# Shared feed-forward units of width 352: 64 columns of gate and of up in one chunk, 32 of each for both halves of the tokens side by side; gathered rows shared out anew

## The reference, cut to what matters

```
x = x + tanh(g_xattn[l]) * xattn_l(layernorm(x), ctx)
x = x + tanh(g_ffn[l]) * ffn_l(layernorm(x))
# ffn of layer 1 (top 4 of 16) and of layer 2 (top 6 of 16): expert width 352, shared width 704
shared = silu(x @ sw_gate) * (x @ sw_up) @ sw_down
routed = sum over the chosen experts e of w_e * (silu(x @ gate_e) * (x @ up_e)) @ down_e
# ffn of layer 0 (top 2 of 16): width 256, gelu, with biases, two shared experts
```

## Time and profile before

| | before |
|---|---|
| median of 3 runs | 2452.13 us (2451.92 to 2452.92) |
| profiled execution | 2452.95 us, its span 2451.2 us |
| PE busy | 2275.7 us, 93% of the span |
| DVE / ACT / POOL busy | 982.8 / 713.6 / 373.9 us |
| mean granted PE clock | 0.973 of full speed |
| stretch of the router stage, layer 1 and layer 2 | 1160.7 to 1219.7, 1591.9 to 1655 us |
| stretch of the combine stage, layers 0, 1, 2 | 763 to 805, 1488 to 1581, 2069 to 2143 us |

### The profile page before, as it was taken

How to read it: one execution, slowest core, us unless ns; L and a number is a source line. 1 busy time by engine, 2 the same in 40 slices (tenths; PEclk the granted TensorE clock), 3 DMA queues, 4 the chain that set the end, 5 groups by cost and what they waited for, 6 DMA issues and landing times. The chain is left out here.

```text
span 2451.2 us, 33056 instructions
## 1 busy us (share of the span) xinstructions
PE 2275.7 (93%) x9625; PEld 1366.0 (56%) x9626; DVE 982.8 (40%) x2525; ACT 713.6 (29%) x1674; POOL 373.9 (15%) x513
## 2 busy tenths in 40 slices
PE   7899999998898899998999999699999999699898
PEld 4444444444664566666456564245656555356587
DVE  5645455444333433335612224771222222602375
ACT  2445353630111566666011110301111110051221
POOL 6100000000122100000011114401111112500061
PEclk9999999998999999999999999799999999899999
DMA  9401010022774100001456555143444452561220
GB/s 345 128 1 35 0 35 0 0 81 95 254 245 137 31 18 6 14 14 53 132 163 201 197 182 168 48 142 111 148 147 148 151 166 78 145 235 38 90 91 31
DMA packets 169969, 263.72 MB, mean 108 GB/s; under 512 B 13134, under 2 KB 106702, under 8 KB 169373
## 3 DMA queue, kind: packets, MB, share of 16 engines
q1 hardware_dynamic: 139869, 186.06, 23.1%
q0 software_dynamic: 15040, 49.30, 6.7%
q10 hardware_dynamic: 14976, 27.27, 2.9%
HBM read 212.78 MB, written 49.81 MB: 107 GB/s over the span
## 5 line engine op out<-in xcount | busy, mean ns | idle before, releaser
L1369 PE MATMUL bank<-f2r_wd,f2b_hT 128*128 (+1 forms) x300 | 137.2, 593 | 1.4 <-DVE f2b_hT L1480 1.4
L1350 PE MATMUL bank<-f2r_wg,f2b_xT 128*128 x400 | 129.2, 467 | 2.0 <-issue 2.0
L1350 PE MATMUL bank<-f2r_wu,f2b_xT 128*128 x400 | 127.0, 460 | 0.0
L1467 DVE TENSOR_TENSOR f2b_h<-bank,f2b_acted 128x352 f32<-128x352 f32 x50 | 26.2, 525 | 203.1 <-PE bank L1350 203.1
L1813 PE MATMUL bank<-l0a_vo,l0a_zT 128*128 128x512 f32 x224 | 101.5, 596 | 3.2 <-DVE l0a_zT L1978 3.2
L1350 PEld LDWEIGHTS bank<-f2r_wu,f2b_xT 128*128 128x128 f32 x400 | 76.4, 191 | 42.8 <-issue 0.7
L1877 ACT ACTIVATE l0a_p<-l0a_p,l0a_low 112x375 f32<-112x375 f32 x128 | 77.2, 607 | 77.5 <-DVE l0a_low L1969 76.4
L1959 DVE CUSTOM_DVE_ANT_0 l0a_p<-bank,xn 112x375 f32<-112x375 f32 x128 | 70.3, 549 | 67.5 <-PE bank L1785 35.6
L1783 PE MATMUL bank<-l_kvcT,xnT 128*112 128x375 f32 x256 | 92.3, 482 | 5.0 <-ACT xnT L1906 5.0
L2154 PEld LDWEIGHTS bank<-l1w_v,ctxT 128*125 128x125 f32 x768 | 88.7, 188 | 8.4 <-issue 0.6
L1350 PEld LDWEIGHTS bank<-f2r_wg,f2b_xT 128*128 128x128 f32 x400 | 73.1, 193 | 35.1 <-issue 4.0
(11 more groups left out here) (410 smaller groups left out, 4281.3 us busy)
## 6 DMA issues: line engine op xcount, KB each, us to landing
slot_rows<-zeros SPq DMA_DIRECT2D x2, 7424.0 KB, 37.7
slot_rows<-f2b_y ACTq DMA_DIRECT2D x50, 256.0 KB, 3.5
f1r_wg<-in_l_wg SPq DMA_DIRECT2D x16, 704.0 KB, 4.3
f1r_wu<-in_l_wu SPq DMA_DIRECT2D x16, 704.0 KB, 5.6
f2r_wg<-in_l_wg SPq DMA_DIRECT2D x16, 704.0 KB, 4.3
f2r_wu<-in_l_wu SPq DMA_DIRECT2D x16, 704.0 KB, 5.6
xn<-in_l_w_ffn SPq DMA_DIRECT2D x11, 768.0 KB, 4.4
l_raw<-in_l_w_ffn SPq DMA_DIRECT2D x11, 768.0 KB, 4.4
```

What stands on the lines that cost most here:

```text
L1350: mm = pe.matmul(bank[:, 0:width], xT[:, v, k, :], w[:, bass.ds(at, 1), k, :].rearrange("p o f -> p (o f)"), start=(k == 0), stop=(k == KD ...
L1369: mm = pe.matmul(bank_y[v][:, :], hT[0:fn, v, c, :], wd[0:fn, bass.ds(at, 1), c, :].rearrange("p o f -> p (o f)"), start=(c == 0), stop=(c ...
```

## The change

The chunk of 96 columns is replaced. Its first 64 columns of the gate and the same 64 of the up lie side by side in one chunk of 128 columns, so that four matmuls make both (a **tail**, one for each half). The last 32 columns of gate and 32 of up make a chunk of 64, and the two halves of the tokens are made in the same four steps: half 0 into partitions 0 to 63 of the bank, half 1 into partitions 64 to 127 (the **rest**, one for both halves). The host lays gate and up out in one array, which is loaded in one transfer where there were two. In layers 1 and 2 there are now 7 pieces: chunk 0 and chunk 1 of half 0, the rest, the tail of half 0, chunk 0 and chunk 1 of half 1, the tail of half 1. The rest needs two activations and two multiplies (of 32 partitions each). Layer 0 keeps its four pieces.

```diff
+        self.whole = whole = width // 128
+        self.pieces = [("chunk", 0, c) for c in range(whole)]
+        if width % 128:
+            self.pieces += [("rest", None, None), ("tail", 0, None)]
+        self.first_half = len(self.pieces)
+        self.pieces += [("chunk", 1, c) for c in range(whole)]
+        if width % 128:
+            self.pieces.append(("tail", 1, None))
+        self.columns = [KD * HALF * (2 if kind == "chunk" else 1) for kind, half, c in self.pieces]
...
+    def make_piece(self, pe, q, gu, h_done, g_done, u_done, between=None):
+        if q >= 2:
+            pe.wait_ge(h_done, q - 1)
...
+        elif kind == "tail":
+            for k in range(KD):
+                mm = pe.matmul(first[:, 0:HALF], gu[:, k, whole * 256:whole * 256 + 128], tokens(k, half),
+                               start=(k == 0), stop=(k == KD - 1))
+            mm.then_inc(g_done, 1)
+        else:
+            for k in range(KD):
+                for half in range(2):
+                    mm = pe.matmul(first[64 * half:64 * half + 64, 0:HALF], gu[:, k, whole * 256 + 128:whole * 256 + 192],
+                                   tokens(k, half), start=(k == 0), stop=(k == KD - 1))
+            mm.then_inc(g_done, 1)
...
+            act.wait_ge(h_done, q)
+            act.activation(acted[64:96, 0, :], bank[0:32, 0:HALF], self.func)
+            act.activation(acted[64:96, 1, :], bank[64:96, 0:HALF], self.func).then_inc(act_done, 1)
...
+            dve.tensor_tensor(hT[64:96, last, 0:HALF], up[32:64, 0:HALF], acted[64:96, 0, :], ALU.mult)
+            dve.tensor_tensor(hT[64:96, last, HALF:NT], up[96:128, 0:HALF], acted[64:96, 1, :], ALU.mult).then_inc(h_done, 1)
```

```diff
+    late = MOST_TILES if top_k > 4 else 0
...
             def product(b):
-                pe.wait_ge(h_done, FC if b < HALF_TILES else PIECES)
+                pe.wait_ge(h_done, FIRST if b < HALF_TILES else PIECES - 1)
...
+                    if b == HALF_TILES and c == FC - 1:
+                        pe.wait_ge(h_done, PIECES)
...
-                columns = 2 * KD * HALF * pieces + FC * D * products
-                return min(len(gathers), len(gathers) * columns //
-                           (2 * KD * HALF * PIECES + FC * D * (HALF_TILES if state else TILES)))
+                columns = sum(shared.columns[:pieces]) + FC * D * products
+                due = len(gathers) - late
+                return min(due, due * columns // (sum(shared.columns) + FC * D * HALF_TILES))
...
             for b in range(HALF_TILES, TILES):
                 add(b)
-                combine_some(share(PIECES, b + 1))
+                if late:
+                    combine_some(added[0] + 1)
```

More of the change, by code:

```diff
@@ L493, in gate_up @@
             def gate_up(q, between=None):
-                half, (f0, fn) = q // FC, chunks[q % FC]
-                if q >= 2:
-                    pe.wait_ge(h_done, q - 1)
-                for weight, out, done in ((wg, s.bank[2 * (q % 2)], g_done), (wu, s.bank[2 * (q % 2) + 1], u_done)):
-                    if between and weight is wu:
-                        between()
-                    for k in range(KD):
-                        mm = pe.matmul(out[0:fn, 0:HALF], weight[:, k, f0:f0 + fn],
-                                       s.xnT[:, k, half * HALF:(half + 1) * HALF], start=(k == 0), stop=(k == KD - 1))
-                    mm.then_inc(done, 1)
+                shared.make_piece(pe, q, gu, h_done, g_done, u_done, between)
             def ranks_and_counts():
@@ L745, in _ @@
                 hidden(q)
[L746 to L747 removed]
+                for i in range(2 * q - 4, min(2 * q - 2, 2 * top_k)):
+                    one_hots(i)
             for i in range(2 * PIECES - 4 if PIECES > 4 else 2, 2 * top_k):
@@ new lines, in __init__, with chunks_until, load @@
+        if width % 128:
[5 more added lines that the diff above has]
+        self.columns = [KD * HALF * (2 if kind == "chunk" else 1) for kind, half, c in self.pieces]
+    def chunks_until(self, q):
+        return sum(kind == "chunk" for kind, half, c in self.pieces[:q + 1])
+    def load(self, eng, i):
+        width, (gu, wd), done = self.width, self.w[i], self.loaded[i]
+        eng.dma_start(gu[:, :, :], self.gate_up[i].rearrange("(k p) f -> p k f", p=128)).then_inc(done, 16)
+        load_down(eng, (None, None, self.w_down), E + i, width, wd, done)
@@ L989, in _ @@
         def _(pe):
[L990 removed]
+            pe.wait_ge(shared.loaded[1], 16 * 3)
             def piece(q):
[L993 to L1000 removed]
+                shared.make_piece(pe, q, gu, h_done, g_done, u_done)
             def product(b):
[L1003 removed]
+                pe.wait_ge(h_done, FIRST if b < HALF_TILES else PIECES - 1)
                 if b >= BANKS:
@@ L1009, in product @@
                 mm.then_inc(y_done, 1)
-            for q in range(FC + 1):
+            for q in range(FIRST + 1):
                 piece(q)
@@ L1016, in _ @@
                 product(b)
-            for q in range(FC + 1, PIECES):
+            for q in range(FIRST + 1, PIECES):
                 piece(q)
-                if state and q == 4:
+                if state and q == FIRST + 1:
                     state.rows_product(pe)
@@ L1120, in _ @@
                 add(b)
-                combine_some(share(FC + 1, b + 1))
-            for q in range(FC + 1, PIECES):
+                combine_some(share(FIRST + 1, b + 1))
+            for q in range(FIRST + 1, PIECES):
                 hidden(q)
-                if state and q == 4:
+                if state and q == FIRST + 1:
                     state.copy_rows(dve)
@@ L2879, in halves_swapped, with shared_parts @@
     return np.ascontiguousarray(w.reshape(w.shape[0], n, 2, width // 2)[:, :, ::-1].reshape(w.shape))
+def shared_parts(width):
+    whole = width // 128 * 128
+    cuts = [0, whole] + ([whole + 64, width] if width > whole else [])
+    return [slice(a, b) for a, b in zip(cuts, cuts[1:])]
 def lay_out(i):
@@ L2937, in lay_out @@
     d["l2_wd"] = c(np.concatenate([f["L2_ffn_w2"].transpose(0, 2, 1), f["L2_ffn_sw2"].T.reshape(2, 352, D)]))
+    for layer in range(3):
+        d[f"l{layer}_shared_gu"] = c(np.concatenate([w[:, :, columns] for columns in shared_parts(d[f"l{layer}_wg"].shape[-1])
+                                                     for w in (d[f"l{layer}_wg"][E:], d[f"l{layer}_wu"][E:])], axis=-1))
     d["l2_decay"] = f["L2_xattn_decay"].reshape(1)
```

133 lines of the change are left out of this document (69 added, 64 removed).

## The result

| | before | changed |
|---|---|---|
| median (20 runs each) | 2452.24 us (2448.48 to 2461.35) | 2459.22 us (2450.59 to 2467.89) |
| profiled execution, its span | 2452.95 us, 2451.2 us | 2457.10 us, 2455.4 us |
| ratio | | 1.0023, 95% interval 1.0013 to 1.0032 |

The forecast was 2451 us and "within 0.2%", its range 2443.5 to 2456.5. The measured time lies 2.7 us above the range, 7.0 us above before.

A forecast was written before the change was run, and what follows sets the result against it. PE, busy 93% of the span, was taken as the bound, with what follows PE deciding the combines of layers 1 and 2. -3.0 - 2.6 + 5.1 + 1.6 - 2.4 = -1.3 us, about 2451 us; range 2443.5 to 2456.5.

The forecast's parts named there:

- combine 0: Layer 0's combine: last product starts earlier and no row is left behind the last piece's, so DVE ends sooner; -2.6 us.
- router 1: Layer 1's router: PE pauses 5.7 us ahead of its first listing, the tail adds 3.0, a slow clock follows; +5.1 us.
- combine 1: Layer 1's combine: PE's last piece ends sooner, so DVE's recurrence begins sooner, with gathers landed by then; -3.0 us.
- router 2: Layer 2's router: PE's saving had in part (-2.9), then tail +3.0, last tables +0.6, clock 0.9; +1.6 us.
- combine 2: Layer 2's combine: with late signals ending at 2123.3 as before, less work lies behind the last product; -2.4 us.
- the hold: Layer 2's combine: signal of PE's finished matmuls some 13 us late, PE standing 11.39 us; assumed to recur once (0.50).
- the hold is gone: Rival, 0.32: no late signal in layer 2's combine, which gathers then bound; stage -7.2, total -6.1, 2446 us.
- held twice: Rival, 0.10: the seventh piece's signal in layer 2's combine also waits for the last gathers; +8.9, total +7.6, 2460 us.
- the clock: Routers: PE runs at half speed behind a pause; +1.6 us in layer 1 (bounds 0 and 3.1), 0.9 in layer 2.
- The rest in 3.0 us: Shared units' rest: narrow matmuls in two groups of output partitions run beside each other, costing 3.0 us, not 6.0.

The follow-up runs named there:

- e3: Kernel before the change, with POOL waiting ahead of gathers 12, 24 and 36 of combine stages until the one before has landed; 2457.41 us, 1.0010 of before.
- e2: Changed kernel, with POOL waiting ahead of gathers 12, 24 and 36 of combine stages until the one before has landed; 2461.51 us, 1.0029 of before.
- e6: e1 with every one-hot table ahead of DVE's table chain, and POOL gaps before gathers 12 and 24 (combine 1) or 20 (combine 2); 2441.96 us, 0.9945 of before.
- e7: e6 with the last two multiplies of layer 2's combine made at once, ahead of the rows that lay between them; 2440.94 us, 0.9945 of before.
- e8: Changed kernel, fetching only the first 64 of 128 rows from the ninth gather of each combine stage on; 2462.06 us, 1.0034 of before.
- e9: Changed kernel, with POOL writing a 64-column tile of zeros behind each gather from the ninth on in combine 1; 1.0038 of before.
- e1: Changed kernel, with the routers' four chunks of 128 ordered ahead of the rest and the two tails; 1.0042 of before.
- e4: Changed kernel, with the old way of sharing out the gathered rows behind the products; 2459.74 us, 1.0026 of before.

## Why the prediction was wrong

Over the traces whose stage is the same program, the mean of each stage moved as follows (before: its two traces, and e3 for the stages that gaps don't touch; changed: its two traces, and the experiments that left the stage alone, six traces for the routers, five for each of the combines of layers 1 and 2).

| stage | forecast | measured | from |
|---|---|---|---|
| combine 0 | -2.6 | -2.8 | 44.1 to 41.3 |
| router 1 | +5.1 | +6.2 | 61.8 to 68.1 |
| combine 1 | -3.0 | +1.0 | 93.9 to 94.8 |
| router 2 | +1.6 | +2.3 | 64.0 to 66.3 |
| combine 2 | -2.4 | -0.4 | 73.5 to 73.0 |
| sum | -1.3 | +6.3 | medians: +7.0 |

The two combines of layers 1 and 2 scatter by 3 to 8 us, so their means are rough; the others are firm within about 1 us.

- **Combine 1, -3.0: this step failed.** It said that the stage "gains what PE gains up to its last piece". PE's work did shrink by 3 us, and with gaps in the gathers the stage does, nearly (91.0, e2, e6, e7). The term that I had put at nothing is what the gathers do to PE in this stage. In seven of the eight traces of the changed combine without gaps, e8 and e9 among them, PE's matmuls were drawn out around the state product (16.4 to 20.7 us from there to the first down product, 14.4 with gaps), and signals came late in all eight and in before's second. I had written that "the same gathers in layer 1 show none", from one trace.
- **Combine 2, -2.4: failed likewise.** The forecast took the hold as a fixed event that ends at 2123.3. It wanders: ahead of the last four products PE stands 11.39 us in before's first trace and 3.67 in its second, and over five traces of the changed stage combine 2 took 70.9 to 78.8 us. Even with one hold, as forecast (the changed kernel's first trace), the stage moved by -1.5: DVE needs 2.5 us for each of the last four tiles (addition, row, statistics), as long as a product, and ended 3.1 us behind the last product, not 2.4. Against "the hold is gone" I argued that three runs agreed within 1.0 us, "so the hold isn't a chance event". Seventeen more runs of before spread over 13 us. The rival "held twice" (10%, 2460 us) is partly what the changed kernel's second trace shows: the seventh piece's signal came 8.8 us late, when POOL had issued its last gather, though the first hold lies at the fourth piece and not at the sixth. That the median, 2459 us, lies next to this rival's is luck: over the traces combine 2 did not get longer.
- **Router 1, +5.1: right in its mechanism, mis-sized in the clock.** The pause was 5.46 us (forecast 5.7), the tail behind it 3.0. The slow stretch cost 3.5 us instead of 1.6; my bound of 3.1 was too low as well, since the listing ahead of the piece runs slowly too. That e1 takes the pause away and finds another one where DVE is late next, and that e6, without either, needs 58.8 us, shows the order to be the cause and not the pieces.
- **Router 2, +1.6 against +2.3: right in its mechanism**, the clock again above what I had taken (the fifth piece's gate took 4.70 us from start to start instead of 3.08, 1.6 lost, forecast 0.9).
- **Combine 0: right**, and e4 gives 2.2 of the 2.8 to the rows.
- **The rest in 3.0 us: right.** Sixteen records took 3.15 us from start to start. The Trainium skill ("TensorEngine Tiling (Array Packing)", section "Tiling Modes") has the engine drain when the mode changes; the wide records on either side were at most 0.1 us further apart than without a change, as the earlier trace rows had said.

So the sum came out 7.6 us low: 4.0 in combine 1, 2.0 in combine 2, 1.1 and 0.7 in the clock of the routers, less 0.2. The first is PE's delay beside the gathers; the second, a difference of means over stages that scatter by 8 us, is the hold as far as I can tell. With the clock alone mis-sized the forecast would have read +0.5, still "no change".

**What was shown and what wasn't.** Shown: with gaps after every twelfth gather the worst delay of a signal is 2.7 us (e2, e3), while each of the ten traces without added gaps has one of 4.7 us or more; gaps also bring combine 1 of the changed kernel to 91.0 us in three kernels out of three; half the data does not (e8). The late signals around a pause of POOL have come 3.4 us after its last issue at the latest; some came while it still issued, and a pause of 2.2 us in e1's combine 1 did not let the state product's signal go (its last matmul ended at 1515.05, the signal came at 1520.75). Not shown: how much of e6's 12 us each of its three edits brings, since no kernel has the new order with the late tables alone. Open: what in POOL's issuing holds PE's signals, why PE's own matmuls are drawn out around the state product of the changed combine 1 and not before the change, and whether a wider step without a full gap would do; e9 didn't reach that.

## What to carry to other kernels

When a change takes work from one engine ahead of a meeting with another, look at who arrives last: work that was cover becomes a pause, and on PE a pause is paid twice, since what follows it runs at half the clock (5.5 us of pause, 3.5 us more). Reordering moves the pause to the next late item of the other engine's chain, so move that engine's items with it: only with all tables ahead of the chain (e6) were both routers no longer than before the change, 58.8 and 63.9 us against 61.8 and 64.0. And one trace is one draw: an unexplained wait that is seen once belongs in the range of every stage with the same ingredients, and wants a second trace before its size goes into a sum.

## What the runs showed of the hardware that I had not expected

- While POOL issues indirect gathers without a break, signals of PE's finished matmuls can arrive 1 to 13 us late. The first such signal belongs to matmuls that ended 13.5 us after the first gather (before's second trace, combine 2) or later (13.7 us in e1's combine 1). It is no fixed rule: combine 1 in the first trace of before had 27 us of gathers and no late signal. With a pause of 3.1 to 3.6 us after every twelfth gather the worst delay was 2.7 us; halving the rows of each gather left one of 6.0 us in combine 1.
- In the changed combine 1 PE's own matmuls were drawn out in the same stretch (3.0 us of work in 6.7), by what the profile calls "issue".
- POOL's step between gathers is 1.25 us with 128 rows and 1.21 with 64, and a 0.17 us write of POOL between two of them made it 1.27.
- Sixteen records of 448 columns, alternately into two groups of 64 output columns, took 3.15 us, where eight of 128 take 3.0.
